# The product with the values of three attentions, in four groups of 32 columns of TensorE's array

## What is computed

```python
scores = jnp.einsum('bhqd,bhkd->bhqk', q, k) / math.sqrt(d_k)
attn = jax.nn.softmax(scores, axis=-1)          # stablemax(scores) in the first
ctx = jnp.einsum('bhqk,bhkd->bhqd', attn, v)    # the product with the values
x = ctx.transpose(0, 2, 1, 3).reshape(B, S, H * dk)
return x @ w_concat.T
```

## Time and profile before

| | us |
|---|---|
| median of three runs | 2549.55 |
| the profiled execution | 2549.83 |
| span of its trace | 2548.1 |
| TensorE busy (matmul / weight loads) | 1638.0 / 1433.4 |
| VectorE, ScalarE, GpSimd busy | 1452.3, 1026.3, 846.2 |
| L1807, the product with the values, busy (3072 matmul records) | 412.8 |
| L1742, fill of the padded values, busy (192 copies) | 45.4 |

### The profile page before, as it was taken

The page is one execution under the profiler, slowest core; times in us unless marked ns, Lnnn a source line. Parts: engine busy times, 40 slices in busy tenths (PEclk is TensorE's granted clock), DMA queues, the critical chain, the costliest instruction groups (busy, mean ns, idle before and its releaser), DMA issues. The chain is left out here.

```text
span 2548.1 us, 40348 instructions
## 1 busy us (share of the span) xinstructions
PE 1638.0 (64%) x10632; PEld 1433.4 (56%) x10632; DVE 1452.3 (57%) x4004; ACT 1026.3 (40%) x2155; POOL 846.2 (33%) x990
## 2 busy tenths in 40 slices
PE   2029925999527887307936999359998366088870
PEld 2029924889516766306925999238887344077660
DVE  4202265532378888601257887758886764077765
ACT  0014414633116666103414777336665133066650
POOL 1455524845320000074511000010000057657771
PEclk9999956999859999558967999569999578588985
DMA  6628722157413221023224331022221021166655
GB/s 189 231 69 233 215 74 78 43 152 215 127 59 96 85 84 43 11 93 91 76 79 113 103 99 53 2 69 80 73 83 34 1 67 55 55 169 181 180 143 173
DMA packets 195285, 259.32 MB, mean 102 GB/s; under 512 B 36992, under 2 KB 148480, under 8 KB 193952
## 3 DMA queue, kind: packets, MB, share of 16 engines
q1 hardware_dynamic: 171744, 208.00, 28.7%
q0 software_dynamic: 23360, 49.20, 5.4%
HBM read 163.12 MB, written 93.97 MB: 101 GB/s over the span
## 5 line engine op out<-in xcount | busy, mean ns | idle before, releaser
L1807 PE MATMUL a_pso<-Y,select 128*128 128x128 f32 x3072 | 412.8, 279 | 4.1 <-ACT Y L1901 2.9
L554 POOL DMA_INDIRECT in_rows<-Y,sent_to x320 | 332.9, 1040 | 239.2 <-issue 99.2
L1807 PEld LDWEIGHTS a_pso<-Y,select 128*128 128x128 f32 x3072 | 379.5, 192 | 22.8 <-ACT Y L1901 10.3
L942 POOL DMA_INDIRECT out_rows<-m_yr,ids x220 | 212.7, 967 | 234.4 <-DVE ids L1126 189.3
L1742 POOL COPY select<-a_vx 128x64 f32<-128x64 f32 x192 | 45.4, 237 | 729.0 <-PE a_pso L1807 706.9
L1069 ACT ACTIVATE m_hf<-m_psu,m_b 128x256 f32<-128x256 f32 x284 | 116.7, 470 | 361.6 <-PE m_psu L1011 361.5
L1024 PEld LDWEIGHTS m_psy<-m_raw,m_hf 128*128 128x128 f32 x1760 | 213.3, 192 | 5.5
L1272 POOL DMA_INDIRECT out_rows<-m_yr,ids x190 | 190.4, 1002 | 76.3 <-issue 49.4
L1786 PE MATMUL a_pss<-a_ring,a_stat 128*128 128x512 f32 x384 | 177.0, 476 | 60.0 <-DMA a_stat<-stat_rows 37.3
L1011 PE MATMUL m_psu<-m_xt,m_raw 128*128 128x256 f32 x880 | 214.1, 387 | 1.8 <-DVE m_xt L1115 1.2
L1024 PE MATMUL m_psy<-m_raw,m_hf 128*128 128x128 f32 x1760 | 213.7, 275 | 0.0
(11 more groups left out here) (258 smaller groups left out, 3578.1 us busy)
## 6 DMA issues: line engine op xcount, KB each, us to landing
select<-in_rows SPq DMA_DIRECT2D x205, 136.0 KB
m_raw<-in_L0f_w SPq DMA_DIRECT2D x41, 512.0 KB, 3.7
m_raw<-in_L0x_w SPq DMA_DIRECT2D x39, 512.0 KB
m_raw<-in_L3f_w SPq DMA_DIRECT2D x99, 192.0 KB
a_ring<-mov_rows SPq DMA_DIRECT2D x576, 32.0 KB
a_stat<-stat_rows SPq DMA_DIRECT2D x72, 256.0 KB, 4.2
in_rows<-xn SPq DMA_DIRECT2D x7, 2448.0 KB, 32.0
n_got<-out_rows SPq DMA_DIRECT2D x24, 512.0 KB, 4.0
```

The costliest lines, as they stand in the source:

```text
L554: pool.indirect_dma_start(k.in_rows[:], bass.IndirectOffsetOnAxis(ap=k.sent_to[:, j, i:i + 1], axis=0), rows[:, i], None).then_inc(sem, 16)
L942: pool.indirect_dma_start(k.out_rows[:], bass.IndirectOffsetOnAxis(ap=k.ids[:, n:n + 1], axis=0), yr[:, b % OUT, i], None).then_inc(y_out[ ...
L1807: last = pe.matmul(pso[j % 2][:, D * o:D * o + D], window, prob[:, j % 2, g, D * (h % 4):D * (h % 4) + D], start=r == 0, stop=r == OCT - 1)
```

## The change

`times_v` does nothing any more for even g. For odd g it does a whole octet. The array is used as four groups of 32 columns: two neighbouring heads share 32 columns, and each matmul has a stationary operand of 32 columns only, and writes 32 partitions of `a_pso`. The first pass takes heads 0, 2, 4 and 6 of the octet, one in each column group, with the start flag; the second takes heads 1, 3, 5 and 7 and adds. The number of matmuls, their moving operands and the contents of `a_pso` are the same; the built program gives each of them a tile of 128 rows by 32 columns at column 0, 32, 64 or 96.

```diff
+    QUARTER = 2 * HR
...
             def times_v(i, j, g):
                 n = batch(i, j)
                 if g % 2 == 0:
-                    pe.wait_ge(padded.sem, padded.done(i * (2 * BODY) + (2 * j + g // 2)))
-                if g == 0:
+                    return
+                o = g // 2
+                pe.wait_ge(padded.sem, padded.done(i * (2 * BODY) + (2 * j + o)))
+                if o == 0:
                     pe.wait_ge(rawtaken.sem, rawtaken.free(n))
                 pe.wait_ge(probs.sem, probs.done(group(i, j, g)))
-                for h in range(4 * g, 4 * g + 4):
-                    o, r = h // OCT, h % OCT
-                    window = vpad[:, o].rearrange("p h w -> p (h w)")[:, D * r:D * r + D]
-                    last = pe.matmul(pso[j % 2][:, D * o:D * o + D], window,
-                                     prob[:, j % 2, g, D * (h % 4):D * (h % 4) + D], start=r == 0, stop=r == OCT - 1)
-                if g == 1:
-                    last.then_inc(octets.sem, 1)
-                if g == GROUPS - 1:
-                    last.then_inc(values.sem, 1)
+                flat_v = vpad[:, o].rearrange("p h w -> p (h w)")
+                for second in range(2):
+                    for quarter in range(4):
+                        r = 2 * quarter + second
+                        h = o * OCT + r
+                        place = (D + HR) * r - HR * second
+                        last = pe.matmul(pso[j % 2][QUARTER * quarter:QUARTER * quarter + QUARTER, D * o:D * o + D],
+                                         flat_v[:, place:place + QUARTER],
+                                         prob[:, j % 2, h // 4, D * (h % 4):D * (h % 4) + D],
+                                         start=second == 0, stop=second == 1)
+                last.then_inc((octets if o == 0 else values).sem, 1)
```

## The result

The changed kernel takes 2557.55 us in the median of eight runs (2553.33 to 2563.00), the kernel before 2551.28 (2547.33 to 2555.38, eight runs). The ratio is 1.0028, 95% interval 1.0016 to 1.0040: 7 us slower by the ratio (6.3 between the medians), with 19 forecast. The profiled execution after took 2561.38 us, its span 2559.6.

A forecast was written before the change was run, and what follows sets the result against it. Second and third attention were taken as bound by a 7.00 us chain per tile, the first not by TensorE; +0.19 and +0.12 make 0.31 us over 62 tiles, 19 us: 2549.83 + 19 = 2569, range 2522 to 2608.

The forecast's parts named there:

- The chain of a tile: Second and third attention: closed chain from VectorE's subtraction through ScalarE, last product, `out` and `add` sets the 7.00 us period.
- The record at 0.055, two at a time: In an octet: a head's two records follow each other, neighbouring heads overlap; records 0.055 apart on average, octet 1.15 us.
- The chain's piece: The last product in a tile's chain, eight narrow heads instead of four whole: 1.15 - 0.96 = +0.19 us.
- rival 1: Octets run four at a time, four rounds of 0.11 plus 0.16: 0.60 us, 2527 us in all; chance 0.29.
- The row with eight moving columns: Norm phase, half clock: records about 0.21 apart, so loading 128 weight columns was taken as a limit of its own.
- The way out: Behind an octet: the next full-width matmul loses 0.16 us, between ends of 0 and 0.27.
- the wait for the octet's last result: The full-width matmul behind an octet waits until its last result is out: 0.275 - 0.11 = 0.16 us.
- The Trainium skill's drain: Rule that a change of tiling mode drains TensorE; by it the 0.16 us is due four times a tile.
- The first octet in front of the fourth transposes: Second and third attention: the first octet delays the fourth transposes and ScalarE's copy behind them, +0.12 us a tile.
- The first attention at 0: First attention: 1.92 us available for an octet of 1.15, so no change, at most a few us either way.
- rival 5: TensorE's clock falls because it is idle more; chance 0.03 together with anything unseen.

The follow-up runs named there:

- wide_a2: Kernel before with the second attention in the new octet order but whole 128-column matmuls: that attention 266.6 us (214.2 before); single run 2747.09 (before 2692.83).
- neigh_a2: Kernel before with 32-column matmuls in the second attention, both heads of a column group directly behind each other: that attention 207.1 us; single run 2674.28 (before 2692.83).
- quad_a2_a3: Kernel before with narrow matmuls in second and third attention, group by group where the whole ones stood: 2668.12 us, ratio 0.9895 (before 2694.09).
- wide_a1: Kernel before with the first attention in the new octet order but whole 128-column matmuls: that attention 244.8 us (227.5 before); single run 2705.12 (before 2692.83).
- a2_a3: Kernel before with the change in second and third attention only, the first as before: 2540.43 us, ratio 0.9951 (before 2550.68).
- twice_a1: Kernel before with 32-column octets in the first attention, each computed twice in a row: that attention 238.0 us (227.5 before); single run 2700.11 (before 2692.83).

## Why the prediction was wrong

The direction was right and the size was not: 7 us against 19, less than half, and within the 7.6 us that the prediction said it could tell. And the direction was right for another reason than the one given. Point by point:

1. **The chain of a tile** was right: `wide_a2` cost 52.4 us where its steps give 50 to 54, and the changed kernel's own steps add up to its 6.77.
2. **The record at 0.055, two at a time**, is the step that failed, and it failed in the second and third attention. "The second record of a head waits until the first has streamed" is not what happens: two heads' records, not one head's, start in each 0.11 us, so a record costs 0.025 to 0.0275, even with four in a row in one column group (`neigh_a2`: 0.027). An octet took 0.58 instead of 1.15. The chain's piece was not +0.19 but -0.38. That was rival 1, at 0.29, with four rounds of 0.11 and an octet of 0.60. The row with eight moving columns had said that the loads are a limit by themselves and would shrink; I gave the moving columns the second word without a row for it.
3. **The way out**: the last of 16 records starts 0.38 after the first, and the next whole matmul comes at 0.57 to 0.58, 0.2 later. The forecast had taken 0.11 + 0.16 = 0.27 for this. It was not the wait for the octet's last result that the forecast had in mind: `out` starts at 1493.01, and the last record's end stands at 1493.07. Two more steps of the chain grew: from the copy to the first product 0.72 instead of 0.66, and from `out` to `add` 0.64 instead of 0.55. The first goes with the octets and not with the narrow matmuls (0.75 in `wide_a2`, 0.63 in `quad_a2_a3`), the second with the narrow matmuls (0.55 in `wide_a2`, 0.64 in `quad_a2_a3`); what causes them was not looked into. Because of them the tile gained 0.23 and not the 0.36 of rival 1. The Trainium skill's drain ("TensorEngine Tiling (Array Packing)", "Key Properties") doesn't contradict the 0.2, which is 0.09 over the 0.11 between whole matmuls; no run separates a drain from the load of the next 128 columns.
4. **The first octet in front of the fourth transposes**, +0.12, did not come: the octet was so short that the scores stood at 1490.36, ahead of the subtraction, and the copy kept its 1.26.
5. **The first attention at 0** is the other step that failed. Its slack was read rightly (1.92 us for an octet that needs 0.64), but rival 5, the clock, was given "little, and no place of its own", since "the first attention has it busy 176.72 of 217 us, at a clock of 1.00". The new load was not similar: TensorE's busy time is 172.67 of 247 us after the change, with a good part of it stretched by the lower clock. Nor does the busy share alone settle the clock: `wide_a1` has the matmuls of before, is busy 204.9 of 245 us, and has 0.92. I should have counted its idle stretches: the tiles with a projection piece had three of 0.64 to 0.86 us already, and the change took the work out from between them. It cost 20 us, and most of the gain of the third attention.

The forecast's 19 us were a loss in the second and third attention that turned out a gain of 10, and a zero in the first that turned out a loss of 20. That the sum came near, and on the same side, is chance.

## What to carry to other kernels

Price a faster matmul by its piece of the chain that closes a step, not by TensorE's busy share: here 412.8 us of busy time fell to 140.3, and the period by 0.23 of 7.00. Ask in the same breath what TensorE does in the time set free. Where another engine bounds a stretch, as in the first attention, faster matmuls give nothing there and can bring the clock down; leave them as they are. And when matmuls are bundled for a shape, keep the places where they stood: the same narrow matmuls group by group gave 26 us where octet by octet they gave 10 (`a2_a3`).

## What the runs showed of the hardware

- f32 matmul records with 32 stationary columns and 128 moving ones start in fours, each four 0.11 us after the last at the full clock and 0.21 at the half (0.0275 and 0.054 a record in `twice_a1`). One record with 128 stationary columns takes 0.11 and 0.21 too. Four records in a row in one column group keep the pace (0.027 in `neigh_a2`).
- From the start of the last 32-column record to the next 128-column matmul 0.2 us pass.
- In the first attention the granted clock was 1.00 where TensorE waited 39 us in all and at most 1.0 at once, 0.68 with 74 us and up to 1.5, and 0.97 with 50 us and up to 1.2, when matmuls whose results are thrown away filled two places. The same 39 us with up to 1.5 at once gave 0.92 (`wide_a1`).
